# Moving the transposes of the next token tile into the last quarter of the gate and up matmuls

## The reference

```python
x = x + attn(layernorm(x), Wq, Wk, Wv, Wo)          # causal, d_k = 128
x = x + ffn(layernorm(x), w_gate, w_up, w_down)

def act_quant(x):                                    # per token
    scale = 127.0 / clip(max(abs(x), axis=-1), 1e-05)
    return clip(round(x * scale), -128, 127) / scale

def ffn(x, w_gate, w_up, w_down):                    # 1024 -> 4096 -> 1024
    gate = silu(act_quant(x) @ quant(w_gate).T)
    up = act_quant(x) @ quant(w_up).T
    return act_quant(gate * up) @ quant(w_down).T
```

## Time and profile before

| | us |
|---|---|
| median of 2 runs | 2597.92 (2596.53 to 2599.31) |
| the profiled execution | 2597.27 |
| its span, slowest core (core 6) | 2595.7 |
| spans of the 8 cores | 2577.5 to 2595.7 |
| TensorE busy in the span | 1721.1 |
| VectorE busy | 943.1 |
| ScalarE busy | 812.6 |

### The profile page before, as it was taken

One profiled execution on the slowest core, in us unless ns is written; L12 is line 12 of the kernel. 1 busy time (PEld: TensorE's weight loads), 2 busy tenths in 40 slices (PEclk: granted clock), 3 DMA queues, 4 the chain that ended last, 5 costly groups with the idle time before them and its releaser, 6 DMA issues.

```text
span 2595.7 us, 25585 instructions; the slowest of 8 cores (2577.5 to 2595.7 us)
## 1 busy us (share of the span) xinstructions
PE 1721.1 (66%) x9618; PEld 886.2 (34%) x9618; DVE 943.1 (36%) x1433; ACT 812.6 (31%) x797; POOL 76.8 (3%) x200
## 2 busy tenths in 40 slices
PE   1333331212222188898889888888988859999999
PEld 1233331112210033343344334433433424444444
DVE  2333336521137634444444444444444420011011
ACT  3333336633432233333333333333333320000000
POOL 1111100000001000000000000000000000000000
PEclk9755555655665599898999999998989979999999
DMA  6666558633348600110111011101101054444443
GB/s 146 189 193 195 194 180 275 218 118 105 100 124 270 231 31 35 41 49 33 41 49 49 33 41 49 49 33 41 49 33 41 33 167 148 155 162 144 149 162 114
DMA packets 74602, 290.08 MB, mean 112 GB/s; under 512 B 10864, under 2 KB 12912, under 8 KB 62192
## 3 DMA queue, kind: packets, MB, share of 16 engines
q1 hardware_dynamic: 42416, 177.29, 22.5%
q10 hardware_dynamic: 19584, 76.55, 7.3%
q0 software_dynamic: 12480, 34.61, 4.4%
HBM read 212.93 MB, written 76.55 MB: 112 GB/s over the span
## 4 chain that ended last, share of the span: by engine, by line
PE 61%; DMA 10%; DVE 9%; ACT 8%; issue 6%; DVEq 4%; POOL 2%; ACTq 0%; POOLq 0%; SPq 0%
PE pb L814 19%; PE pb L821 18%; PE pb L945 17%; DMA wdqh<-wdq_st 5%; DVE h_sb L833 3%; ACT kres L831 3%; DVEq L754 2%; DMA nqt_sb<-wgt 1%; ACT nqh_sb L284 1%; ACT wdq_st L420 1%; DMA x_st<-x 1%; PE pb L504 1%; PE pb L479 1%; PE pb L306 1%; DVEq L409 1%
## 5 line engine op out<-in xcount | busy, mean ns | idle before, releaser
L814 PE MATMUL pb<-wgq,qres 128*128 128x512 bf16 x2048 | 816.6, 399 | 165.3 <-DVE qres L795 130.8
L821 PE MATMUL pb<-wuq,qres 128*128 128x512 bf16 x2048 | 814.6, 398 | 0.0
L945 PE MATMUL pb<-wdq_sb,nqt_in 128*128 128x512 bf16 x2048 | 444.6, 380 | 23.0 <-DMA nqt_in<-nqh 23.0
L833 DVE SCALAR_TENSOR_TENSOR h_sb<-pb,st_cols,kres 128x1024 f32<-128x1024 f32 x128 | 164.3, 1284 | 627.9 <-ACT kres L831 627.9
L814 PEld LDWEIGHTS pb<-wgq,qres 128*128 128x128 bf16 x2048 | 208.5, 102 | 435.1 <-issue 220.4
L821 PEld LDWEIGHTS pb<-wuq,qres 128*128 128x128 bf16 x2048 | 207.9, 102 | 258.3 <-issue 42.3
L945 PEld LDWEIGHTS pb<-wdq_sb,nqt_in 128*128 128x128 bf16 x2048 | 200.9, 98 | 266.5 <-issue 26.6
L831 ACT ACTIVATE kres<-pb,st_cols 128x1024 f32<-128x1024 f32 x128 | 142.7, 1115 | 369.2 <-PE pb L821 205.7
L504 PE MATMUL pb<-qres,kres 128*128 128x128 bf16 x528 | 51.9, 258 | 240.3 <-ACT pt L522 225.9
L769 ACT ACTIVATE nqh_sb<-h_sb,konst 128x4096 bf16<-128x4096 f32 x32 | 118.7, 3709 | 234.4 <-DVE h_sb L766 234.4
L955 DVE SCALAR_TENSOR_TENSOR out_sb<-pb,c_all,x_in 128x512 f32<-128x512 f32 x32 | 24.0, 751 | 431.8 <-PE pb L945 431.8
(11 more groups left out here) (155 smaller groups left out, 1498.1 us busy)
## 6 DMA issues: line engine op xcount, KB each, us to landing
nqh<-nqt_sb ACTq DMA_DIRECT2D x32, 1024.0 KB, 3.9
nqt_in<-nqh SPq DMA_DIRECT2D x32, 1024.0 KB, 6.1
x_st<-x POOLq DMA_DIRECT2D x38, 512.0 KB, 6.3
x_st<-x1h SPq DMA_DIRECT2D x32, 512.0 KB, 3.3
x_in<-x1h SPq DMA_DIRECT2D x32, 512.0 KB, 7.2
y<-out_sb ACTq DMA_DIRECT2D x32, 512.0 KB, 7.3
wstage<-x POOLq DMA_DIRECT2D x26, 512.0 KB, 5.7
nqh_sb<-wdt SPq DMA_DIRECT2D x19, 512.0 KB, 5.8
```

What stands on the lines that cost most here:

```text
L814: tt = sc.op('t', (lambda c=c, o0=o0, gb=gb, half=half, par=par: (lambda e: e.matmul(gb[:, half * 512:(half + 1) * 512], xqTb[par][:, c * ...
L821: tt = sc.op('t', (lambda c=c, o0=o0, ub=ub, half=half, par=par: (lambda e: e.matmul(ub[:, half * 512:(half + 1) * 512], xqTb[par][:, c * ...
L833: v_stt_q[(i, qtr)] = sc.op('v', (lambda qtr=qtr, ub=ub, i=i: (lambda e: e.scalar_tensor_tensor(h_sb[:, qtr * 1024:(qtr + 1) * 1024], ub, ...
L945: tt = sc.op('t', (lambda c=c, half=half, par=par: (lambda e: e.matmul(dps[par][:, half * 512:(half + 1) * 512], nqt_in[par][:, c * 128:(c ...
```

## The change

The A block becomes a function, `emit_Ablock(j)`, with the same instructions and the same waits. It is issued for tile 0 ahead of the loop, and for tile i+1 inside quarter 3 of tile i, ahead of the matmuls of chunk c = 2, that is after 8 of the quarter's 32 matmuls. The ychain of tile i is issued at the end of iteration i and no longer after the A block of tile i+1. The value of the copy is kept in an array for quarter 0.

```diff
-    for i in range(NT):
-        par = i % 2
-        qpair = [0, 1, 1, 0] if i % 2 == 0 else [1, 0, 0, 1]
-        fpair = 0 if i % 2 == 0 else 1
-        apair = i % 2
-        gbank = {0: pb[0], 1: pb[2]}
-        ubank = {0: pb[1], 1: pb[3]}
+    v_xqt_arr = [0] * NT
+    gbank = {0: pb[0], 1: pb[2]}
+    ubank = {0: pb[1], 1: pb[3]}
+
+    def emit_Ablock(j):
+        apair = j % 2
         aps = pb[0] if apair == 0 else pb[2]
-        tw = [('S', s_xq[i]), dq_const,
+        tw = [('S', s_xq[j]), dq_const,
               ('S', pair_free[apair][0]), ('V', pair_free[apair][1])]
-        if i == 0:
+        if j == 0:
             tw += [('V', v_otev_g[NT // GRP - 1]), ('V', v_x1add[NT - 1])]
         tt = 0
         for c in range(HC):
@@ -788,14 +787,19 @@
                 aps.bitcast(BF16)[:, c * 128:(c + 1) * 128],
                 xq2[:, c * 128:(c + 1) * 128], ident)))(),
                 waits=tw if c == 0 else (), inc='T')
-        t_xqA[i] = tt
+        t_xqA[j] = tt
         vw = [('T', tt)]
-        if i < 2:
+        if j < 2:
             vw += [ds_x1[NT - 2], ds_x1[NT - 1], ds_wd_done]
-        v_xqt = sc.op('v', (lambda par=par, aps=aps: (lambda e: e.tensor_copy(
-            xqTb[par], aps.bitcast(BF16)[:, 0:1024])))(), waits=vw, inc='V')
-        if i >= 1:
-            emit_ychain(i - 1)
+        v_xqt_arr[j] = sc.op('v', (lambda j=j, aps=aps: (lambda e: e.tensor_copy(
+            xqTb[j % 2], aps.bitcast(BF16)[:, 0:1024])))(), waits=vw, inc='V')
+
+    emit_Ablock(0)
+    for i in range(NT):
+        par = i % 2
+        qpair = [0, 1, 1, 0] if i % 2 == 0 else [1, 0, 0, 1]
+        fpair = 0 if i % 2 == 0 else 1
+        v_xqt = v_xqt_arr[i]
 
         for qtr in range(4):
             pr = qpair[qtr]
@@ -809,6 +813,8 @@
             first = True
             tt = 0
             for c in range(HC):
+                if qtr == 3 and c == 2 and i + 1 < NT:
+                    emit_Ablock(i + 1)
                 for half in range(2):
                     o0 = qtr * 1024 + half * 512
                     tt = sc.op('t', (lambda c=c, o0=o0, gb=gb, half=half, par=par: (lambda e: e.matmul(
@@ -874,7 +880,7 @@
                 ds_nq[i - 1] = ('DSN', v2)
             if qtr == 1 and i + 1 < NT:
                 chain_blk2(i + 1)
-    emit_ychain(NT - 1)
+        emit_ychain(i)
```

## The result

The changed kernel takes 2628.15 us (median of 7 runs) where the kernel before takes 2597.4 in the same rounds: a ratio of 1.0117, 95% interval 1.0104 to 1.013. That is slower by 30.7 us, within 2%. In some executions of each of these kernels a few cores or a whole die run at a lower granted clock, as in one of the seven here (2814.58 us, die 0 at a mean of 0.75 against 0.82), and the ratios leave executions as slow as this one out. The forecast was 2604 in a range of 2588 to 2638. The profiled execution has a span of 2621.1 us on its slowest core, core 3; all numbers of the kernel after are from that core unless another is named.

The account below looks back on a forecast made before the run. TensorE was taken as busiest, stopped by waits and low clock, at 37.48 us per tile. Full-clock 35.37 - 4.81 + 5.65 + 0.41 = 36.62, plus 1.1 for the clock, gave 37.72: +7 us over 31 tiles, 2604 us, range 2588 to 2638.

Parts of the forecast that it names:

- The wait taken away: At the tile boundary: quarter 0 follows quarter 3 directly, so the whole gap of 4.81 us per tile goes.
- The wait added: Inside quarter 3, after 8 matmuls: the A transposes wait for line 742 (s_xq), a hole of 5.65 us, some 5.0 idle.
- What is late next: Between quarters 1 and 2: the ychain's path loses its cover, so the gap grows from 2.96 to 3.37 us, +0.41.
- The full-clock tile: One tile's time without clock loss: 35.37 us before, 36.62 after, with +0.84 and +0.41.
- The clock: Low-clock work behind the new hole: 1.1 us per tile, between ends of 0.4 and 2.1, against 2.11 before.
- the longer hole swallows more of whichever stretch comes: Inside quarter 3: low-clock time lying in the idle hole costs nothing, the reason for taking 1.1 us, below the middle.
- the three costs that the prediction worked out: Behind the hole: 3.42 us stretch beginning at 2.4 costs 0.4, beginning at 5.0 costs 1.7; the long stretch costs 2.1.
- the clock costs what it did: Rival: 2.11 us per tile behind the new hole, tile 38.73, 2636 us; chance 0.18.
- second fall: Rival, between quarters 1 and 2: clock falls there too, 1.71 us more per tile, 2657 us; 0.08, shared with longer low stretch.
- The rule of the Trainium skill: Gap between quarters 1 and 2: transposes don't count as clock activity like matmuls, making 3.37 us an idle hole; 2657 us.
- The rival of the hole that "isn't there": Quarter 3: xq ready by the ninth matmul, only 0.45 us of transposes stay, -6.06 us per tile, 2409 us; chance 0.05.

Follow-up runs that it names:

- early_xq_c2: Changed kernel, A block still ahead of chunk 2, with block 3 of the next tile issued after quarter 1, behind block 2: 2453.18 us, ratio 0.9425.
- late_c7: Changed kernel with the A block ahead of chunk 7 in place of chunk 2: 2430.22 us, ratio 0.9356 to the kernel before.
- early_xq_c4: Changed kernel with block 3 of the next tile issued after quarter 1 and the A block ahead of chunk 4: 2402.99 us, ratio 0.9249.

## Why the prediction was right, and which term was not

*The wait taken away.* Right: quarter 0 follows quarter 3 without a wait on the copy, so 4.81 us per tile went.

*The wait added.* Right, to 0.1 us: the transposes start 6.92 us after quarter 3 begins, a hole of 5.65 by the same sum (idle 5.03, forecast "some 5.0"; 157.1 us in all, forecast about 155). early_xq_c2 shows that `s_xq` is its cause, and late_c7 that the 24 matmuls queued behind it are its price.

*What is late next.* The mechanism was right and a little too dear: the gap between quarters 1 and 2 grew by 0.14 to 0.16 us (2.96 to about 3.11) and not by 0.41, so it stayed under the 3.3 to 3.5 that was to show it. The chain ran 0.25 faster than its walk, since line 769's end and the next silu overlap by 0.1, the multiply of quarter 1 follows the reduce 0.09 closer, and the silu of quarter 3 starts 0.27 after the boundary and not 0.32. The new wait of line 862, 0.34 us in the tile shown, stayed off the path, as the prediction had it.

The full-clock tile was forecast at 36.62 and is about 36.35 to 36.4: +1.0 us against before.

*The clock.* This term was mis-sized: 1.1 us per tile forecast, 2.2 measured, as in the kernel before. The step that failed is "the longer hole swallows more of whichever stretch comes". It took the low stretch to end at most 9.2 us after the idle time began, since no row of before ended later. In the changed kernel the one of 1550.87 ends at 1561.88, 11.0 after. Of the three costs that the prediction worked out, two came as they stood: 1.7 for a short stretch that begins at the hole's end (1.68), and 2.1 for a long one that begins 2.4 us into it (2.12). The third, 0.4, came in none of the 31 tiles; in its place a long stretch begins some 4.2 us into the hole and costs 3.0. On core 3 a fall costs from 1.3 to 3.0 us, with the same mean as before. So the case called "the clock costs what it did", with a chance of 0.18 and 2636 us, is what happened, and with the gap at its true size it gives +1.0 x 31 = 31 us: 2628. The two errors, +0.27 and -1.1 per tile, had opposite signs, so it is in part luck that the forecast was only 24 us low. The time lies in the range because its upper end took the clock's term at 2.1.

*The rivals.* From the second tile on no second fall came between quarters 1 and 2: the low stretches of all 8 cores begin in the hole or just behind it. A window over that gap, and the loop, whose clock is the 0.93 that was forecast, both on core 3:

```profile
1654.85:1657.96 3.11, 2.12 (x34) 1.84 (x34) 2.92 (x4) 1.73 (x3) 0.00 (x0) 1.00 0.53 169
906.00:2101.50 1195.50, 1003.69 (x5176) 476.24 (x5177) 509.12 (x704) 426.54 (x276) 0.00 (x0) 0.93 0.11 40
```

The rule of the Trainium skill that was weighed (TensorE: Matmul & The Clock Gate, Part 4: PE-mode transpose) would have allowed one; with a gap of 3.1 us, 32 transposes in it, the trace doesn't agree. early_xq_c4 has the same gap, late_c7 one of 2.96, and both a mean clock of 1.00 over the loop. The first tile makes the comparison: there are no transposes of h yet, TensorE is idle for 2.80 us between quarters 1 and 2 on every core, and on four of the eight cores (0, 2, 5 and 6) the clock falls. On core 0, the wait, and then its window and the work behind it:

```profile
927.07 0.58 PE L820 MATMUL pb<-wgq,qres 128*128 128x512 bf16 x1 [2.80 <-DVE h_sb L839]
```

```profile
924.27:927.07 2.80, 0.01 (x1) 0.03 (x1) 1.33 (x2) 1.11 (x1) 0.00 (x0) 0.86 0.00 0
927.07:929.70 2.63, 2.63 (x7) 0.96 (x8) 2.45 (x3) 0.00 (x0) 0.00 (x0) 0.50 0.03 6
```

So a gap of this length, when empty, can make the clock fall, and it never did with the 32 transposes in it. The first tile also differs in what stands before it, a stretch of low clock that ends at 912.7 on core 0, so the transposes' part is likely but not shown alone.

The rival of the hole that "isn't there" left out a wait. Its 2409 us took xq to be ready at the ninth matmul and nothing else to be missing; early_xq_c2 built that and needs 2439 to 2442, since the bank is free only after the multiply of quarter 2. Only with the block ahead of chunk 4 as well is nothing waited for: 2403.

## What to carry to other kernels

Before work of the next tile is put ahead of work of this one in a queue that runs in order, compare two times in the trace: when the queue gets there, and when the operand is ready. A wait costs the work behind it; here 5 us of wait moved from one place to another, while its place further back (2430 us) or its producer further ahead (2403 us, with the block ahead of chunk 4) gained 6.4 and 7.5% against the kernel before. When an engine waits for a copy, look first at what stands ahead of that copy in its own engine's queue.

## What the runs showed of the hardware

What the clock costs goes by the number of falls far more than by the length of the hole. Behind idle holes of 5.0 us and more it fell in all 31 tiles, behind 3.3 us in 23 to 31 of them, behind 2.45 us in 5 on core 3, behind 0.75 us in none, and the mean cost of a fall stayed between 2.0 and 2.9 us from 3.3 to 6.76 us, without an order in the length. Bringing a hole of 3.3 us down to 2.45 therefore gained 102 us (2591 to 2489) where the full-clock sums differ by 0.86 x 31 = 27. Behind the three equal holes of 5.03 us the time at low clock ran from 3.36 to 5.98 us, so one tile read alone misleads; the mean over the loop is the number to use. An empty gap of 2.80 us in the first tile made the clock fall on four of eight cores, a gap of 3.11 us with 32 transposes in it on none.
